# Deformable sampling on one core: coordinates spread by DMA, hats of 64x64, a second fold on GpSimd

## The reference

```
om = conv3x3(x, w_off) + b_off              # 27 channels: off_y, off_x, mask logits
py = off_y + y + ky ; px = off_x + x + kx   # 9 taps k
s[c,k,y,x] = mask * bilinear(x[c], py, px)  # zero outside the image
out = sum_{c,k} w[o,c,k] * s[c,k,y,x] + b
out = relu(batchnorm(out)) + x
```

## Time and profile before

| | |
|---|---|
| median of 3 runs | 1183.15 us (1178.95 to 1183.35) |
| profiled execution, own time | 1181.56 us |
| its span, first to last instruction | 1179.8 us |
| mean granted TensorE clock | 0.965 of full |
| busy: PE, PEld | 1079.9 us (92%), 824.4 us (70%) |
| busy: DVE, ACT, POOL | 864.1 (73%), 810.5 (69%), 551.9 us (47%) |
| DMA moved | 22.51 MB, mean 19 GB/s |

### The profile page before, as it was taken

How to read it: one execution, slowest core, us unless ns; L and a number is a source line. 1 busy time by engine, 2 the same in 40 slices (tenths; PEclk the granted TensorE clock), 3 DMA queues, 4 the chain that set the end, 5 groups by cost and what they waited for, 6 DMA issues and landing times.

```text
span 1179.8 us, 26432 instructions
## 1 busy us (share of the span) xinstructions
PE 1079.9 (92%) x7562; PEld 824.4 (70%) x7562; DVE 864.1 (73%) x1037; ACT 810.5 (69%) x1496; POOL 551.9 (47%) x432
## 2 busy tenths in 40 slices
PE   4778888789996799999999999999999999999983
PEld 2435555433445688888878888878888888888873
DVE  2379999843436377777777777777777778888885
ACT  1347767511122688888878888888888888888865
POOL 1028788342232144555555445544554455555540
PEclk9689999999998899999999999999999999999996
DMA  3000000043211100000000000000000000000001
GB/s 121 0 1 1 0 0 0 1 92 82 57 45 43 18 10 12 14 10 9 12 15 12 9 10 14 11 11 11 15 11 9 10 10 3 4 4 2 2 3 71
DMA packets 53391, 22.51 MB, mean 19 GB/s; under 512 B 44750, under 2 KB 51412, under 8 KB 53076
## 3 DMA queue, kind: packets, MB, share of 16 engines
q1 hardware_dynamic: 52924, 21.46, 7.5%
q10 hardware_dynamic: 408, 0.25, 0.1%
HBM read 10.25 MB, written 7.01 MB: 15 GB/s over the span
## 4 chain that ended last, share of the span: by engine, by line
PE 80%; DVE 10%; issue 6%; ACT 1%; DMA 1%; DVEq 1%; POOL 1%; ACTq 0%; POOLq 0%
PE PS L1157 79%; DVE region L672 2%; DVE region L628 2%; DMA bcol<-in_boff 1%; DVE region L632 1%; DVE region L647 1%; DVE region L634 1%; PE PS L1227 1%; DVE region L617 1%; DVE region L629 1%; PE PS L1425 0%; DVE region L785 0%; DVE two L880 0%; DVE region L614 0%; ACT region L1151 0%
## 5 line engine op out<-in xcount | busy, mean ns | idle before, releaser
L1157 PE MATMUL PS<-region 128*128 (+4 forms) x5504 | 717.0, 294 | 17.7 <-POOL region L436 7.3
L1157 PEld LDWEIGHTS PS<-region 128*128 128x128 f32 (+1 forms) x5504 | 629.6, 182 | 109.6 <-issue 78.8
L821 DVE TENSOR_TENSOR region<-PS,region 128x1296 f32<-128x1296 f32 x256 | 386.0, 1508 | 163.5 <-PE PS L1157 163.4
L525 POOL TENSOR_TENSOR region<-region 128x576 f32<-128x576 f32 x256 | 307.5, 1201 | 363.6 <-DVE region L821 363.6
L1077 ACT ACTIVATE region<-x 64x576 f32<-64x576 f32 x512 | 349.1, 682 | 30.2 <-ACT x L1073 0.8
L1073 ACT ACTIVATE x<-PS,cst 128x640 f32<-128x640 f32 x256 | 202.3, 790 | 89.1 <-PE PS L1157 88.9
L833 DVE TENSOR_REDUCE region<-region 128x720 f32 (+1 forms) x256 | 228.6, 893 | 2.8 <-POOL region L525 2.8
L1157 PE MATMUL PS<-region,selb 6*128 6x320 bf16 (+1 forms) x512 | 106.5, 287 | 0.0
L1157 PE MATMUL PS<-region,woff 128*108 (+3 forms) x192 | 88.6, 605 | 0.8 <-DVE xp L750 0.8
L431 POOL TENSOR_TENSOR region<-region,cst 128x1024 f32<-128x1024 f32 x32 | 61.6, 1926 | 49.8 <-ACT region L953 25.3
L672 DVE SCALAR_TENSOR_TENSOR region<-region,wr (+4 forms) x57 | 73.9, 1297 | 0.1
(11 more groups left out here) (136 smaller groups left out, 802.4 us busy)
## 6 DMA issues: line engine op xcount, KB each, us to landing
two<-xr_scratch SPq DMA_DIRECT2D x300, 16.0 KB, 1.7
xr_scratch<-region SPq DMA_DIRECT2D x8, 384.0 KB
region<-xp SPq DMA_DIRECT2D x10, 264.0 KB, 4.4
out<-region SPq DMA_DIRECT2D x4, 512.0 KB, 3.0
px_scratch<-region SPq DMA_DIRECT2D x64, 27.0 KB
region<-px_scratch SPq DMA_DIRECT2D x64, 27.0 KB
region<-xp SPq DMA_DIRECT2D x6, 280.5 KB, 4.5
x<-in_x SPq DMA_DIRECT2D x1, 1536.0 KB, 10.7
```

The lines of the kernel that those rows point to most:

```text
L525: pool.tensor_tensor(uu[:, r % 4, :, 0:FOLD], uu[:, r % 4, :, 0:FOLD], uu[:, r % 4, :, NA - FOLD:NA], ALU.add).then_inc(fold_ready, 1)
L821: v.tensor_tensor(uu[:, u4].rearrange("p o (b a) -> p b o a", b=3), PS[:, 3 * u:3 * u + 3, 0:432].rearrange("p b (a o) -> p b o a", o=C), ...
L1157: return nc.tensor.matmul(o, l, r, start=start, stop=stop)
```

## The change

- TensorE no longer spreads coordinates. SP stores the fp32 coordinates themselves (in the order sample, row, tap, column) and reads them back with a broadcast to 64 partitions, two rows at a time and sample (`load_px`), into a ring of eight rows `px`. The split of the coordinates, `selb` and the clearing of `wt` go.
- The hat is compact: `wt` is 128 x 9 x 64, made by one activation. A tap is two matmuls of 64x64, on partitions 0 to 63 and 64 to 127.
- The image slots come in rounds of 3, 3 and 2 rows, before taps 0, 3 and 6, into banks 6 and 7 in turn, with one copy of a round on ScalarE.
- GpSimd folds twice: 36 terms, then 18, the second waiting for the first. VectorE reduces 27 terms instead of 45, of row n - 2 instead of n - 1. At a pair's end two sums stand in a row.
- VectorE's write to `two` and the first two stagings wait for the stores (`px_done`). TensorE's loop over chunks within a pair is written out.

```diff
@@ sync @@
-                    sp.wait_ge(lo_ready, done(n))
+                    sp.wait_ge(om_out, done(n, 2))
                     for b in range(B):
                         row, h = OC * (b % PAIRS) + KK, b // PAIRS
-                        sp.dma_start(px_dram[b, :, :, bass.ds(n * CH, CH)].rearrange("s k c -> k s c"),
-                                     spl[row:row + KK, u, :, h * CH:(h + 1) * CH]).then_inc(px_stored[u], 16)
+                        sp.dma_start(px_dram[b, bass.ds(n * RPC, RPC)].rearrange("r k c -> k r c"),
+                                     two[row:row + KK, u, h * CH:(h + 1) * CH].rearrange("p (r c) -> p r c", c=W)).then_inc(px_stored[u], 16)
...
+            def load_px(g, y, line):
                 for h in range(2):
+                    sp.dma_start(px[W * h:W * (h + 1), line:line + GR, :].rearrange("p r a -> p (r a)"),
+                                 px_dram[bass.ds(g + h * PAIRS, 1), bass.ds(y, GR)].rearrange("b r k c -> b (r k c)").to_broadcast([W, GR * KK * W])
+                                 ).then_inc(px_in[line // GR], 16)
...
+                def chunk(g, c, rows, after):
+                    s = g * NCH + c
+                    if rows:
+                        sp.wait_ge(slot_ready, 3 * s + 2)
+                        load_rows(s + 1, g + 1, c, c % 2)
+                    if after is not None:
+                        for line in range(0, RPC, GR):
+                            sp.wait_ge(wt_ready, done(s * RPC + line + GR - 1))
+                            load_px(after[0], after[1] * RPC + line, line)
@@ gpsimd, tables_ahead @@
-                                               uu[:, r % 4, :, NA - FOLD:NA], ALU.add).then_inc(fold_ready, 1)
+                                               uu[:, r % 4, :, NA - FOLD:NA], ALU.add).then_inc(half_ready, 1)
+                            pool.wait_ge(half_ready, s * RPC + r + 1)
+                            pool.sem_inc(pool_turn, 1)
+                            pool.tensor_tensor(uu[:, r % 4, :, 0:FOLD // 2], uu[:, r % 4, :, 0:FOLD // 2],
+                                               uu[:, r % 4, :, NA - FOLD - FOLD // 2:NA - FOLD], ALU.add).then_inc(fold_ready, 1)
@@ vector @@
-                    dve.wait_ge(rest_ready, free(n))
+                    dve.wait_ge(px_done, free(n))
...
+            dve.wait_ge(px_done, done(NCH - 2))
             stage(0, 0)
+            dve.wait_ge(px_done, done(NCH - 1))
             stage(1, 1)
...
-                        v.tensor_reduce(total(y, g), uu[:, u, :, 0:NA - FOLD], AX.X, ALU.add).then_inc(os_ready, 1)
+                        dve.wait_ge(os_ready, n + 2)
+                        v.tensor_reduce(total(y, g), uu[:, u, :, 0:NA - FOLD - FOLD // 2], AX.X, ALU.add).then_inc(os_ready, 1)
...
-                            if r > 0 or not isinstance(c, int) or c > 0:
-                                add(s * RPC + r - 1, c * RPC + r - 1, (r - 1) % 4)
+                            if r > 1 or not isinstance(c, int) or c > 0:
+                                add(s * RPC + r - 2, c * RPC + r - 2, (r - 2) % 4)
                     chunks(chunk)
+                    add(g * H + H - 2, H - 2, 2)
                     add(g * H + H - 1, H - 1, 3)
@@ scalar, row @@
-                act.wait_ge(bc_ready, done(n))
-                a.activation(ab[:, u, :].rearrange("p (b a) -> p b a", b=2), PS[:, 6:8, 0:PXA], ACT.Abs, bias=c_("negx")).then_inc(ab_ready, 1)
+                if line % GR == 0:
+                    act.wait_ge(px_in[line // GR], 32 * loads)
+                a.activation(px[:, line, :], px[:, line, :], ACT.Abs, bias=c_("negx")).then_inc(ab_ready, 1)
                 act.wait_ge(t_ready, free(n))
                 act.wait_ge(ab_ready, done(n))
-                for h in range(2):
-                    a.activation(wt[W * h:W * (h + 1), u, :, W * h:W * (h + 1)],
...
+                a.activation(wt[:, u].rearrange("p k s -> p (k s)"), px[:, line, :], ACT.Relu, bias=1.0, scale=-1.0).then_inc(wt_ready, 1)
@@ tensor @@
+            def slot_round(q, b, u, bank):
+                pe.wait_ge(row_out, free(q))
+                for r in range(3 * b, 3 * b + ROUNDS[b]):
                     for h in range(2):
+                        at = KK * C * (r - 3 * b)
+                        ins = mm(PS[W * h:W * (h + 1), bank, at:at + KK * C], xrow[:, u, r, h, :], wsp[0:SPLITS * C, :])
+                ins.then_inc(slot_ready, 1)
+            def taps(n, u, rows_of):
+                pe.wait_ge(wt_ready, done(n))
                 pe.wait_ge(u_ready, free(n))
+                pe.sem_inc(pe_turn, 1)
                 for k in range(KK):
+                    for h in range(2):
+                        half = slice(W * h, W * (h + 1))
+                        ins = mm(PS[half, 3 * u + k // 3, 144 * (k % 3):144 * (k % 3 + 1)], wt[half, u, k, :], rows_of(k)[half])
```

More of the change, by code:

```diff
@@ L1110, in chunk @@
                         for r in range(RPC):
-                            slot = TOP + H - RPC + r if first else None if last else c * RPC + (TOP - RPC + r)
-                            row(s * RPC + r, r % 2, slot)
+                            row(s * RPC + r, r, s + 1, r % 2)
+                            if r in (2, 5, 7) and (first or not last):
+                                b = (2, 5, 7).index(r)
+                                slots_out(3 * s + b, (TOP + H - RPC if first else c * RPC + TOP - RPC) + 3 * b, b, 6 + (u + b) % 2)
                             if r in (4, 6) and not (last and end):
@@ L1382, in chunk @@
                             n = s * RPC + r
-                            if r < RPC - 1:
-                                px(n + 1, u * RPC + r + 1, (1 - u, r + 1) if here else None, here)
-                            elif not (last and end):
-                                pe.wait_ge(px_ready, s + 2)
-                                if not last:
-                                    pe.wait_ge(xr_ready, s + 2)
-                                px(n + 1, (1 - u) * RPC, (u, 0) if not last else None, here)
-                            taps(n, c * RPC + r, r % 2, None)
-                    chunks(chunk)
+                            if here and r in (0, 3, 6):
+                                if r == 0:
+                                    pe.wait_ge(xr_ready, s + 1)
+                                slot_round(3 * s + r // 3, r // 3, 1 - u, 6 + (u + r // 3) % 2)
+                            taps(n, r % 2, lambda k, y=c * RPC + r: img4[:, k, y + k // 3:y + k // 3 + NR, :])
+                    for c in range(NCH):
+                        chunk(c, c % 2)
                 stream(pe, pair)
@@ L1399, in sample @@
                 pe.wait_ge(im_out, (p * NCH + 2 * NCH + LAST) * 3)
-                pe.wait_ge(px_ready, p * NCH + 1)
-                px(p * H, 0)
-                def two_chunks(step, end):
-                    for r in range(2 * RPC):
-                        y = step * 2 * RPC + r
-                        if not (end and r == 2 * RPC - 1):
-                            if r % RPC == RPC - 1:
-                                pe.wait_ge(px_ready, p * NCH + 2 * step + r // RPC + 2)
-                                pe.sem_inc(pe_turn, 1)
-                            px(p * H + y + 1, (r + 1) % (2 * RPC))
-                        taps(p * H + y, y, r % 2, band)
-                with pe.Fori(0, H // (2 * RPC) - 1) as step:
-                    two_chunks(step, False)
-                two_chunks(H // (2 * RPC) - 1, True)
+                pe.wait_ge(band_ready, p + 1)
+                pe.sem_inc(pe_turn, 1)
+                with pe.Fori(0, H // RPC) as step:
+                    for r in range(RPC):
+                        y = step * RPC + r
+                        taps(p * H + y, r % 2, lambda k: band_rows[:, k, :])
             branches(pe, sample_all, sample)
```

138 lines of the change are left out of this document (51 added, 87 removed).

## The result

The changed kernel takes 1071.15 us (median of 4 runs, 1069.6 to 1072.2) against 1181.05 for the kernel before, measured beside it: a ratio of 0.907, 95% interval 0.904 to 0.909. The profiled execution has a span of 1069.3 us, against 1179.8, so 110.5 us have gone.

The account below looks back on a forecast made before the run. TensorE was taken to bound three pairs (2.43 us a row), GpSimd the last (2.36). Gains of 96, 24, 4 and 2.7 us less 0.5 made 126 off 1181.56: 1055, as median 1057; range 1030 to 1100.

Parts of the forecast that it names:

- TensorE's bound, and its row of 2.93 us: Sampling rows of the kernel before: TensorE, busy throughout, sets each row at 2.93 us, 2.74 in the last pair.
- Taps of 64x64 at 62 ns a record: TensorE's taps after the change: both halves overlap fully, 36 records at 62 ns, 2.23 us a row.
- Rival C: TensorE's taps: the two 64x64 halves do not overlap, 4.66 us a row, 1617 us in all; chance 0.11.
- Slot rounds, 0.20 us a row: TensorE's image-slot matmuls in three rounds per eight-row chunk: 1.7 us per chunk, 0.20 a row.
- GpSimd, 2.36 us: GpSimd's row: folds 1.20 and 0.72, wait 0.10, tables 0.34; under TensorE in three pairs, over it in the last.
- rival B: Sampling rows: GpSimd sets every one at 2.54 us, 94 us gained, 1088 us in all; chance 0.20.
- VectorE hidden at 2.08: VectorE's row with the sum over 27 values: 2.08 us, hidden behind the bound, as even 2.40 would be.
- ScalarE 1.8, hidden: ScalarE's row with one hat activation fewer: some 1.8 us from about 2.5, hidden.
- DMA hidden at 120 GB/s: Coordinate broadcasts in sampling: 590 KB per two rows in 4.9 us, 120 GB/s, hidden with 144 GB/s taken as reachable.
- rival D: Coordinate loads: DMA sets the pace at 92 GB/s, 3.2 us a row, 1257 us in all; chance 0.05.
- Ahead of the loop, 6.7 us: Before the sampling loop: 4 us gained by dropping the coordinate split, 2.7 us on the first row's way.
- nothing, at worst 1 us three times: Ends of pairs, two last sums before the next product: no loss, at worst 1 us three times.

## Why the prediction was right, and where it was off

**TensorE's bound, and its row of 2.93 us:** right; both folds laid on the kernel before change nothing (1.000).

**Taps of 64x64 at 62 ns a record:** right, 62.0 measured in the last pair. Issued in turn, the halves overlap in full. The rule weighed against it, from the Trainium skill, "TensorEngine Tiling (Array Packing)", section "Gotcha 1: PSUM Pressure", does not bite here: both halves write one bank at the same time, on partitions of their own, at full speed. Rival C named a real place all the same. The overlap hangs on the order in which the halves are issued, and with nine taps of one half in a row the time is 2294 us, above the 1617 worked out, since the clock falls as well. The page of the Trainium skill "TensorE: Matmul & The Clock Gate", section "The mechanism", says that matmuls start and end strictly in program order. By that, halves apart could overlap with one record at each change of halves, and they did with some 4; and halves two and two would have cost some 360 us, and took 4. If a start is the beginning of the streaming, the rule doesn't hold for groups of four records.

**Slot rounds, 0.20 us a row:** too dear. With one fold of 40 terms TensorE's row is 2.365 with slots and 2.204 without, 0.16 for the rounds; the forecast had 2.43 and 2.23.

**GpSimd, 2.36 us:** this is the step that failed, in two terms of its sum. The second fold was put at 0.72 and took 0.816; the wait for its own result at 0.10, from a copy, and took 0.18. Together with the tables 2.476, inside the bounds of 2.24 and 2.54, but on the other side of TensorE's row. So the forecast's split, TensorE in three pairs and GpSimd in the last, was wrong: GpSimd sets all 256 rows, which is rival B's mechanism at a somewhat lower price. That it would be over TensorE in the last pair was right. That the forecast is only 14 us off is partly luck: with TensorE's row as measured its own split would have given 192 x 0.065 = 12 us less, about 1045, so an engine priced too dear made up for one priced too cheap. The range held because its upper end had been drawn for B as well.

**VectorE hidden at 2.08, "and even 2.40 would be":** the 2.08 right, and by more than I gave it, since successive instructions overlap by 0.08 us; of the 2.40, which is the row with one fold, right in three pairs, while in the last VectorE sets it. The overlap is what makes the second fold a loss: one fold leaves VectorE at 2.224, under TensorE's row with slots (2.365) and only 0.02 over its row without. The tight place at the chunk's end, "the product waits some 0.3": there, and longer, 1.8 us a chunk on average, because GpSimd is behind.

**ScalarE 1.8, hidden:** right. 0.761 + 0.684, the slot copies and tables; it is the engine that the compact hats relieve, and without them it sets the row at 2.56.

**DMA hidden at 120 GB/s:** right, 4.3 us to landing with rows to spare. I took 144 GB/s as reachable; 223 was reached in the last pair of the run with every load twice. At twice the traffic DMA does hold up the row, in three pairs by way of SP's queue and not by the rate of rival D.

**Ahead of the loop, 6.7 us:** 10.6 measured. The staging came at 363.67, 8 us earlier instead of 4. The late next was the one named: the second staging waits for SP's stores, 1.9 us before 366.86.

**Between pairs, "nothing, at worst 1 us three times":** wrong. The gaps are longer by 2.0, 3.4 and 2.7 us, 8 together, of which 3 are left when the last rows of each pair, with no table to wait for and so a little faster, are set against them. I priced the sums at the pair's end for a GpSimd that keeps up. It runs behind: in the first and third place the next product waits for the last sum, and that 2.71 us for the second fold, with a mask product before it. The kernel before with both folds shows much of the same, 4.7 us in all. In the second place TensorE is late; there I had left out that the written-out loop makes its pause longer, 3.62 us for 1.6, and that the granted clock is down to 0.61 behind it.

**The sum:** the forecast had 126 us. The rows gave 104.6 (192 x 0.453 + 64 x 0.275) where it had 120, the way to the loop 10.6 for 6.7, the tail cost 1.5 for 0.5, and the pairs' ends 3.2 for nothing: 110.5 in all.

## What to carry to other kernels

When one engine is relieved, compare the rows of all the others to within 0.1 us before giving one of them more work: here the change without its second fold is worth 145 us, 106 of them from taking the spreading off TensorE and the rest from the compact hats, which relieve ScalarE, and the fold added beside it gives 33 back. A sum of mean durations overstates an engine whose instructions overlap, and understates one whose instructions wait for each other's results. Two half-sized matmuls for one whole cost nothing here while they were issued in turn or in groups of four records, and a great deal in groups of 18.

## What the runs showed of the hardware

- 64x64 fp32 matmuls of 144 columns on opposite quarters of the array, issued in turn, keep 62.0 ns a record, half of the 124 that a 128x128 record takes.
- In groups of four records a half the same matmuls still overlap (4 us more in all); in groups of 18 only some 4 records at each change do, the others are 240 ns apart, and the granted clock stays at 1.2 GHz, 0.50, for the whole stretch, although TensorE counts as busy throughout.
- GpSimd: an addition of 128x288 takes 0.816 us where one of 128x576 takes 1.204, and a wait for its own last result 0.18.
- Broadcasts from DRAM in pieces of 4.6 KB, 288 KB each, run at 130 GB/s beside everything else and at 223 when more are asked for (share 1.03); 16 KB loads queued among twice as many of them took 11.3 us to land for 2.1.
- Where TensorE's loop jumps back over 64 written-out rows, it stands still for over 3 us and then has a granted clock of 0.56 for 3.5 us (34 records, where 4.0 us at the full clock had 69); with the pairs written out as well the pause is 1.19 us and the clock stays at 1.00.
